# Eight more output steps on GpSimd, another tile order in one chunk of two, and two reorderings behind the attention loop

## The reference

```python
x = x + attn(layernorm(x))     # 16 heads of width 32, split in two halves of 16: a = a1 - lam * a2
x = x + ffn(layernorm(x))      # two linears with ternary weights, relu(h)**2 between them
# in attn, after a @ v:
rms = jnp.sqrt(jnp.mean(out * out, axis=-1, keepdims=True) + EPS)
out_n = out / rms * norm_w * (1.0 - LAMBDA_INIT)
# out_n is regrouped and multiplied by wo
```

## Time and profile before

| | us |
|---|---|
| median of 3 runs (lowest to highest) | 3753.06 (3751.36 to 3754.15) |
| the profiled execution | 3751.29 |
| its span, first to last instruction | 3749.6 |
| PE / DVE / ACT / POOL busy | 3705.7 / 3151.7 / 2793.5 / 616.0 |
| start of pair 0, end of pair 63 | 103.72, 2750.50 |

### The profile page before, as it was taken

How to read it: one execution, slowest core, us unless ns; L and a number is a source line. 1 busy time by engine, 2 the same in 40 slices (tenths; PEclk the granted TensorE clock), 3 DMA queues, 4 the chain that set the end, 5 groups by cost and what they waited for, 6 DMA issues and landing times.

```text
span 3749.6 us, 57714 instructions
## 1 busy us (share of the span) xinstructions
PE 3705.7 (99%) x21736; PEld 2054.5 (55%) x21736; DVE 3151.7 (84%) x2918; ACT 2793.5 (75%) x3626; POOL 616.0 (16%) x281
## 2 busy tenths in 40 slices
PE   7999999999999999999999999999999999999999
PEld 6444444444444444444444444444468888888887
DVE  6899999999999999999999999988875555555554
ACT  4788888898888888888888888889863333333333
POOL 0101001023434344223222301320010000000000
PEclk9999999999999999999999999999999999999999
DMA  7544444444444544454555444544340101010010
GB/s 246 124 104 105 98 106 104 109 99 106 108 95 103 111 103 98 111 118 101 111 110 121 95 100 105 124 95 114 78 152 23 45 23 45 23 45 23 29 40 23
DMA packets 255351, 344.58 MB, mean 92 GB/s; under 512 B 118000, under 2 KB 142576, under 8 KB 254000
## 3 DMA queue, kind: packets, MB, share of 16 engines
q1 hardware_dynamic: 251504, 324.43, 36.4%
q0 software_dynamic: 3392, 15.73, 1.3%
q10 hardware_dynamic: 128, 0.03, 0.0%
HBM read 198.55 MB, written 131.07 MB: 88 GB/s over the span
## 4 chain that ended last, share of the span: by engine, by line
PE 88%; DVE 7%; issue 3%; ACT 1%; DMA 1%; ACTq 0%; DVEq 0%; SPq 0%
PE ps L886 22%; PE ps L861 16%; PE ps L955 13%; PE ps L1013 12%; PE ps L799 9%; DVE acc L1651 5%; PE ps L941 5%; PE ps L802 4%; PE ps L909 3%; PE ps L960 2%; PE ps L771 1%; PE ps L1049 1%; PE ps L1034 1%; PE ps L922 1%; ACT pr L1281 1%
## 5 line engine op out<-in xcount | busy, mean ns | idle before, releaser
L1281 ACT ACTIVATE pr<-ps 128x1024 f32<-128x1024 f32 x2048 | 1990.1, 1029 | 258.5 <-PE ps L861 252.5
L1651 DVE TENSOR_TENSOR acc<-acc,pr 128x2048 f32<-128x2048 f32 x768 | 1782.0, 2320 | 40.7 <-ACT pr L1281 10.8
L886 PE MATMUL ps<-pr,vst 128*32 128x512 f32 x8192 | 1011.1, 600 | 0.0
L861 PE MATMUL ps<-qst,kst 50*128 50x512 f32 x4096 | 782.2, 457 | 10.4 <-ACT pr L1281 7.5
L861 PEld LDWEIGHTS ps<-qst,kst 50*128 50x128 f32 x4096 | 337.7, 184 | 657.5 <-ACT pr L1281 457.3
L886 PEld LDWEIGHTS ps<-pr,vst 128*32 128x32 f32 x8192 | 213.5, 109 | 445.6 <-issue 436.4
L1450 ACT ACTIVATE rb<-ps,scf 128x512 f32<-128x512 f32 x228 | 157.1, 689 | 349.9 <-PE ps L960 349.9
L1013 PE MATMUL ps<-tP,hh_ 128*128 128x512 f32 x1024 | 399.7, 390 | 2.8 <-DVE hl_ L1872 2.8
L1013 PE MATMUL ps<-tP,hl_ 128*128 128x512 f32 x1024 | 398.9, 390 | 0.0
L799 PE MATMUL ps<-xt,wqh 128*128 128x512 f32 x1024 | 379.4, 422 | 2.2 <-DVE xt L1541 2.1
L477 POOL TENSOR_SCALAR xin<-xin,mv,rs 128x512 f32<-128x512 f32 x60 | 208.0, 3470 | 877.0 <-DVE rs L1570 877.0
(11 more groups left out here) (179 smaller groups left out, 3814.2 us busy)
## 6 DMA issues: line engine op xcount, KB each, us to landing
qst<-q_scratch SPq DMA_DIRECT2D x128, 256.0 KB, 4.7
kst<-k_scratch SPq DMA_DIRECT2D x128, 256.0 KB, 7.0
q_scratch<-stg SPq DMA_DIRECT2D x112, 256.0 KB
k_scratch<-stg SPq DMA_DIRECT2D x112, 256.0 KB
qst<-q_scratch SPq DMA_DIRECT2D x128, 128.0 KB, 4.9
kst<-k_scratch SPq DMA_DIRECT2D x128, 128.0 KB, 7.7
vst<-v_scratch SPq DMA_DIRECT2D x128, 128.0 KB, 4.7
xr<-in_L_attn_x_dram SPq DMA_DIRECT2D x64, 256.0 KB
```

What stands on the lines that cost most here:

```text
L861: ins = e.matmul(ps[:, 2 * c + hh, :], kst[rows, r, j, t * 128:(t + 1) * 128], qst[rows, r, j, c * 512:(c + 1) * 512], start=True, stop=True)
L886: ins = e.matmul(ps[32 * c4:32 * c4 + 32, 4 + j, :], vst[:, r, t, 32 * hh:32 * hh + 32], pr[:, sl, c, hh, :], start=(t == 0), stop=(t == 7 ...
L1281: e.activation(pr[:, sl, c, :, :], ps[:, 2 * c:2 * c + 2, :], ACT.Exp, scale=SCALE).then_inc(s_exp, 1)
L1651: e.tensor_tensor(acc[:, j, :], old, new, ALU.add).then_inc(s_add, 1)
```

## The change

- `POOLED` gains the pairs 19, 23, 27, 31, 35, 39, 43 and 47. Their join stands in POOL's program of pair X+1 behind `pool_magnitudes` or `pool_ternary` and ahead of `pool_part_apply`. The other three operations stand at the end of POOL's work of pair X+1.
- The odd chunks from the third on take their tiles in another order: their four pairs hold 2, 2, 3 and 1 tiles of q or k (before 2, 3, 3 and 0). The flag steps move back by one double step.
- SP loads the rows of tile 0 of the feed-forward part after the output steps of pair 62, instead of ahead of them. POOL issues four loads ahead of `dg`, instead of seven.

```diff
-ORDER = ((0, 1, 8, 2, 3, 9, 4, 5, 10, 6, 7, 11), (0, 1, 8, 2, 3, 4, 5, 6, 7, 9, 10, 11))
+ORDER = ((0, 1, 8, 2, 3, 9, 4, 5, 10, 6, 7, 11), (0, 1, 8, 2, 3, 9, 4, 5, 6, 7, 10, 11),
+         (0, 1, 8, 2, 3, 4, 5, 6, 7, 9, 10, 11))
-POOLED = (LOWP - 2, LOWP - 1, LOWP)
+POOLED = (19, 23, 27, 31, 35, 39, 43, 47, LOWP - 2, LOWP - 1, LOWP)
-    return C, ORDER[C % 2][i]
+    return C, ORDER[C % 2 if C > 1 else 2 * C][i]
@@ gpsimd_program
                 if PROJ_P <= P < PROJ_P + 16:
                     pool_ternary(e, P - PROJ_P)
+                if P < LOWP - 2 and P - 1 in POOLED:
+                    join_halves(e, P - 1)
                 pool_part_apply(e, P)
                 if SUM_P <= P < PROJ_P:
                     pool_magnitudes(e, 2 * (P - SUM_P) + 1)
+                if P < LOWP - 2 and P - 1 in POOLED:
+                    pool_normed(e, P - 1)
...
-            for uu in range(7):
+            for uu in range(4):
                 pool_load_up(e, uu)
...
-            for uu in range(7, NUP):
+            for uu in range(4, NUP):
@@ sync_program
-            sync_rows(e, 0)
             sync_post(e, NPAIR - 2, 13)
             sync_post(e, NPAIR - 2, 16)
             sync_post(e, NPAIR - 1, 13)
+            sync_rows(e, 0)
             sync_rows(e, 1)
@@ tensor_program
-                        if d == 2:
+                        if d == 3:
                             pe_flag(e, P // NP + 1)
-                        if d == 4:
+                        if d == 5:
                             flag = load_flag(e, P // NP + 1)
@@ vector_program
-                        if q == NP - 1 and P + 1 < NPAIR and (d, half) in ((1, 1), (3, 0)):
-                            dve_flag(e, P // NP + 1, d // 2)
+                        if q == NP - 1 and P + 1 < NPAIR and (d, half) in ((2, 1), (3, 0)):
+                            dve_flag(e, P // NP + 1, d - 2)
```

## The result

The changed kernel takes **3805.97 us** (median of 4 runs, 3805.01 to 3807.02) against 3753.32 for the kernel before. The ratio on record is **1.0146**, 95% interval 1.0134 to 1.0159; the quotient of the two medians is 1.0140. So it is about 1.4% to 1.5% slower. The forecast was 3798, with a range of 3768 to 3822. The profiled execution took 3805.01 us.

What follows compares the result with a forecast made beforehand. PE, busy 99% of the span, was taken as the bound. 3751.3 + 38.4 (joins) + 15.5 (clock) - 5.5 (DVE relief) - 1.35 (behind the loop) = 3798.3, about 3798 us; range 3768 to 3822.

Steps and rivals of the forecast that it cites:

- The join: In eight pairs, POOL's join ends after PE wants `ot`; PE waits 4.6 or 5.0 us, together 38.4.
- the long one in the earlier trace: Join on POOL before the change that took 3.40 us, having begun just after a DVE addition of 2.29.
- The clock: Half speed expected on PE after each of the eight waits: 15.5 us together, bounds 0 and 31.
- The rate of 1.94 us: Cost assumed per half-speed stretch, from pair 2's 43.04 us against a plain pair's 41.10.
- The rival in which the clock holds: Joins are late but PE's clock stays at full speed after the waits: 3783 us, chance 0.23.
- The relief of DVE: Pairs 17 to 48: new tile order and DVE's dry stretches should return 5.5 us, bounds 0 and 6.8.
- the 6.8 us of excess: Time of pairs 17 to 48 above plain and last pairs, taken as all a lighter DVE could return.
- It takes 1.35 us of DVE work from the second pair of an odd chunk to its last: Tile-order step: moving this DVE work within odd chunks should help return most of 6.8 us; 5.5 taken.
- a bound of 2.7 over seven batches: Flag moved by one double step, in the batches' last pairs: taken as 0, bounds -2.7 and +2.7 us.
- POOL's other three operations: Scaling, copy and low part on POOL: hidden from PE, effect on DVE taken as 0, bounds -4 to +4 us.
- Behind the loop: With the 1 MB load later, PE's 1.35 us pause goes: -1.35 us, bounds 0 and -2.

Runs made afterwards that it cites:

- experiment 2: The changed kernel with the eight joins still on POOL but ahead of the weight instructions of their pair: 3750.11 us, ratio 0.9996 to the kernel before.
- experiment 4: The changed kernel with 20 unused matmuls put before PE's wait for the late join in each of the eight pairs: 3787.44 us, ratio 1.0096.
- experiment 5: The changed kernel with each of the eight joins one instruction earlier on POOL, between second and third weight instruction: 3775.08 us, ratio 1.0057.
- Experiments 1: The changed kernel with only the eight joins given back to DVE, the other three operations staying on POOL: 3749.46 us, ratio 0.9995.
- experiment 3: The changed kernel with none of the eight pairs on POOL, tile order, flag steps and both reorderings kept: 3749.65 us, ratio 0.9997.

## Why the prediction was right

**The join: right, in place and size.** The forecast said 4.6 us of idle PE in pair 20 and 5.0 in pair 36; the trace has 4.59 and 4.81, ended by the join on POOL in all eight pairs, and 37.5 us in all where 38.4 were forecast. The join took 3.31 us in pair 20, as the long one in the earlier trace rows, and 1.29 with no DVE addition in the way (experiment 2). The addition delayed it as forecast (it ended 1.12 us behind the addition, where 1.27 was assumed). The kernel lost the wait nearly one for one: 36.3 of 37.5 us by experiment 4.

**The clock: right in kind, too small.** 15.5 us were forecast, and experiment 4 gives 19.3, inside the bounds of 0 and 31. The rate of 1.94 us came from a short stretch at half speed in pair 2, taken against a plain pair of 41.10. But pair 2 itself takes 41.54 to 41.58 us in the ten kernels here in which no such stretch falls in it, so the short stretch cost it 1.5, in line with the 1.6 of experiment 5. After the long waits the half speed lasts longer (951.90 to 956.50 is all at 0.50), and it costs 2.4 us each. The price of a short stretch was set too high and the stretches were taken as short; in part these made each other good, which was luck. The rival in which the clock holds did not occur in any pair of the changed kernel.

**The relief of DVE: wrong, and this is the largest miss.** The forecast returned 5.5 of the 6.8 us of excess in the pairs 17 to 48. Pairs 22 and 30 did fall to 41.12, but 23 and 31, forecast at 41.1 to 41.5, rose to 42.58 and 42.66. Together the pairs there without a join or a batch's end returned 2.5, but the batches' last pairs took 2.8 (forecast: 0, with a bound of 2.7 over seven batches). The step that failed is "It takes 1.35 us of DVE work from the second pair of an odd chunk to its last", read as if the last pair could carry it at no cost. DVE was at 40.24 of 41.97 us there and went to about 41.8. The 6.8 us were also never one store that a lighter DVE could empty: 2.9 lay in the eight pairs with a join, 1.0 in the four last pairs and 2.9 in the others. Experiments 1 and 3 show 331.8 us for the pairs with a join, with and without POOL's help, so even without the late join nothing would have come of their share.

**POOL's other three operations: right.** They were taken as 0, and experiments 1 and 3, with and without them, take 3749.46 and 3749.65 us.

**Behind the loop: right.** -1.35 us forecast, -1.7 measured, and the pause is gone. It was SP's reordering that removed it.

The sum by measured terms: 3751.3 + 36.3 + 19.3 + 2.8 - 2.5 - 1.7 = 3805.5, and -0.5 for the rest (ahead of the loop and in all other pairs) gives the 3805.0 of the profiled run. The forecast was 7 us low: 4 by the clock, 6 by the relief that did not come, less 2 by the wait.

No version tried here is faster than the kernel before by more than the measurement can tell. With the join ahead of the weight instructions, the change is worth nothing measurable: 0.9996 (0.9987 to 1.0005).

## What to carry to other kernels

Before an operation is moved to a less busy engine, find the time at which its result is wanted and the times at which the instructions ahead of it in the new engine's order end. GpSimd was busy 16% of the span, and that said nothing about the 4.6 to 4.8 us by which it was late eight times. On a PE that hardly ever pauses, a wait costs its length, and it can cost the half clock behind it as well (here half as much again). And a lighter pair is no gain where the pair was plain already: look at which pairs exceed the plain time before taking work out of them.

## What the runs showed of the hardware

A wait of only 1.85 us of PE was followed by half clock, as were all but one of the 16 waits of 1.85 to 4.81 us in the changed kernel and in experiment 5. The pause of 1.35 us was not. But the length of the wait does not settle it. In pair 1 of the kernel before, where the clock falls just before pair 2, PE's last waits are far shorter:

```profile
184.79 0.51 PE L861 MATMUL ps<-qst,kst 50*128 50x512 f32 x2 [0.65 <-ACT pr L1281]
185.80 0.75 PE L861 MATMUL ps<-qst,kst 50*128 50x512 f32 x2 [0.50 <-ACT pr L1281]
```

The kernel of experiment 3 has the same waits there (0.65 and 0.50 us), and its clock stays at 1.00. What else decides is left open. And 160 matmuls of no use, put into the waits, took back 15 to 20 us by keeping the clock at 1.00 (15.5 us by the medians, each against its own kernel before; 19.3 in the eight pairs of the profiled executions).
